# Mixture-of-experts layer of a fused decoder block: dense experts, or rows routed to slots by expert

## The reference

```
x = x + attn(layernorm(x))            # 16 heads of 64, 8 pooled "agent" queries a sequence
x = x + xattn(layernorm(x), ctx)      # 16 heads of 8, causal
x = x + ffn(layernorm(x))             # routed and shared experts
```

```
scores  = softmax(xf @ gate_w.T)                # 16 experts in 4 groups
idx     = the 2 best experts within the 2 best groups; weights = their scores
h       = silu(xf @ We1[e] + be1[e]) * (xf @ We3[e] + be3[e])       # 128 -> 64, an expert e
y       = sum over the 2 chosen e of weight * (h @ We2[e] + be2[e]) # 64 -> 128
z       = silu(xf @ ws1 + bs1) * (xf @ ws3 + bs3) @ ws2 + bs2       # shared, 128 -> 128 -> 128
return y + z
```

## Time and profile before

| what | value |
|---|---|
| median of 3 runs | 1166.43 us (1164.69 to 1166.88) |
| the profiled execution: its time, its span | 1165.22 us, 1163.5 us |
| busy in the span | PE 84%, PEld 66%, VectorE 68%, ScalarE 50%, GpSimd 20% |
| granted TensorE clock, mean | 0.921 |
| chain that ended last | PE 55%, VectorE 25%, ScalarE 12% |
| moved by DMA | 18.36 MB, 16 GB/s over the span |

### The profile page before, as it was taken

The page is one execution under the profiler, slowest core; times in us unless marked ns, Lnnn a source line. Parts: engine busy times, 40 slices in busy tenths (PEclk is TensorE's granted clock), DMA queues, the critical chain, the costliest instruction groups (busy, mean ns, idle before and its releaser), DMA issues.

```text
span 1163.5 us, 22091 instructions
## 1 busy us (share of the span) xinstructions
PE 975.4 (84%) x9023; PEld 768.2 (66%) x9069; DVE 791.6 (68%) x1841; ACT 576.3 (50%) x1148; POOL 227.7 (20%) x220
## 2 busy tenths in 40 slices
PE   6656889969897889978899698978899788996687
PEld 5543678737785577846787486855777477864566
DVE  3256866687766976678666877669766877568454
ACT  5335645357434664357453574346643574445322
POOL 6001410035000520024100340005200231004200
PEclk9896989979999999979899799989999899997789
DMA  5300010000100010000100000000100000000000
GB/s 145 78 1 1 2 37 1 10 10 6 33 10 10 2 37 1 10 10 2 37 10 1 10 26 13 10 10 2 37 1 10 11 2 1 10 2 10 1 1 19
DMA packets 28902, 18.36 MB, mean 16 GB/s; under 512 B 7649, under 2 KB 27394, under 8 KB 28802
## 3 DMA queue, kind: packets, MB, share of 16 engines
q1 hardware_dynamic: 26914, 12.48, 4.1%
q0 software_dynamic: 1280, 4.20, 1.2%
q10 hardware_dynamic: 608, 0.27, 0.1%
HBM read 12.62 MB, written 4.19 MB: 14 GB/s over the span
## 4 chain that ended last, share of the span: by engine, by line
PE 55%; DVE 25%; ACT 12%; POOL 3%; issue 3%; SPq 1%; DMA 0%; another core or an unknown queue 0%; DVEq 0%; POOLq 0%
PE banks L510 8%; PE banks L491 5%; PE banks L674 5%; PE banks L492 4%; PE banks L493 4%; DVE mx L1219 3%; PE banks L648 3%; PE banks L624 3%; DVE PXUT L1220 3%; ACT M L865 3%; PE banks L606 3%; PE banks L767 2%; DVE lx L1231 2%; PE banks L541 2%; DVE sil L1164 2%
## 5 line engine op out<-in xcount | busy, mean ns | idle before, releaser
L872 ACT ACTIVATE sil<-banks,b 128x512 f32<-128x512 f32 x144 | 99.6, 691 | 219.0 <-PE banks L493 216.8
L510 PE MATMUL banks<-w,hT 128*128 128x128 f32 x1152 | 156.8, 280 | 25.4 <-DVE hT L1171 22.8
L510 PEld LDWEIGHTS banks<-w,hT 128*128 128x128 f32 x1152 | 154.0, 196 | 22.2 <-DVE hT L1171 12.9
L1164 DVE SCALAR_TENSOR_TENSOR sil<-banks,b,sil 128x512 f32<-128x512 f32 x128 | 95.9, 749 | 103.1 <-ACT sil L872 94.2
L865 ACT COPY M<-banks 128x512 f32<-128x512 f32 x208 | 123.0, 609 | 81.0 <-PE banks L624 64.9
L389 POOL DMA_DIRECT2D out_x<-xn x16 | 12.9, 809 | 551.6 <-DVE xn L1177 551.6
L426 POOL TENSOR_TENSOR PXUT<-PXUT,rx 128x512 f32<-128x512 f32 x80 | 87.2, 1117 | 102.1 <-DVE rx L1233 102.1
L1171 DVE TENSOR_TENSOR hT<-sil,banks 128x512 f32<-128x512 f32 x128 | 87.9, 687 | 17.9 <-PE banks L500 11.4
L624 PE MATMUL banks<-ident,PXUT 128*128 128x128 f32 x384 | 64.4, 308 | 29.8 <-ACT M L865 24.0
L598 PE MATMUL banks<-maskb,pick 32*64 32x512 bf16 x512 | 45.0, 487 | 47.1 <-ACT PXUT L928 28.2
L624 PEld LDWEIGHTS banks<-ident,PXUT 128*128 128x128 f32 x384 | 45.4, 154 | 52.4 <-ACT M L865 34.2
(11 more groups left out here) (199 smaller groups left out, 2046.6 us busy)
## 6 DMA issues: line engine op xcount, KB each, us to landing
xin<-in_x SPq DMA_DIRECT2D x8, 512.0 KB, 4.2
cin<-in_ctx SPq DMA_DIRECT2D x8, 512.0 KB, 5.4
out_x<-xn POOLq DMA_DIRECT2D x16, 256.0 KB, 2.8
KQ<-in_L_attn_Wqkv SPq DMA_DIRECT2D x3, 512.0 KB, 5.3
KQ<-in_L_ffn_We SPq DMA_DIRECT2D x2, 512.0 KB, 4.5
KQ<-in_L_attn_Wo SPq DMA_DIRECT2D x1, 512.0 KB, 8.0
w<-in_L_ffn_We SPq DMA_DIRECT2D x1, 512.0 KB
woM<-xwT SPq DMA_DIRECT2D x16, 8.0 KB, 1.8
```

The costliest lines, as they stand in the source:

```text
L510: mm(ps(name)[:, P * t:P * t + P], hT[:, k % 2, P * t:P * t + P], w2[:, pair[k], :], start=(n == 0 and t == 0), stop=False, skip_group_che ...
L872: nc.scalar.activation(sil[:, k % 2, :], ps(f"H1_{k}")[:], ACT.Silu, bias=b1[:, pair[k]:pair[k] + 1]).then_inc(sil_ready, 1)
L1164: V.scalar_tensor_tensor(sil[:, k % 2, :], ps(f"H3_{k}")[:], b3[:, p:p + 1], sil[:, k % 2, :], ALU.add, ALU.mult).then_inc(hid_ready, 1)
```

## The change

The expert layer is computed for the chosen tokens only, and is spread over four rounds. The calls become `both(e, g, f, h)`, 11 of them: `g` is the attention's group, `e` one group behind (gate, shared experts, ranks), `f` two behind (experts), `h` three behind (sum).

For group `e`: the three-way split, `weight` and the dense units are removed. The shared experts are two fp32 chunks. `ranks` makes, by products with a triangle and with ones, each token's rank among its expert's tokens; `positions` on VectorE (16 linked instructions or so) turns these into a row number in a buffer of 32 slots of 128 rows, and into the expert of each slot (`ids`). GpSimd scatters `xn3` in 16 indirect DMAs of 128 rows to the buffer `xs_d` in HBM.

For group `f`: four units of 8 slots. SyncE reads each slot's expert from SBUF into a register and starts two DMAs by it (64 KB of `w13_d`, 33 KB of `w2b_d`), then loads the unit's rows (512 KB) and later stores the results (512 KB). TensorE turns the rows, multiplies (two slots share the array: 64 output rows each, then 64 input rows each), ScalarE and VectorE make silu and product on 128x128 pieces.

For group `h`: GpSimd gathers each token's two results in 16 indirect DMAs, VectorE adds them with their weights to `base`, which SyncE had stored and loads again.

```diff
-    UNITS = CHUNKS * (EP + 1)
+    SLOTS = TOPK * TOK // P + E
+    UNIT = 8
+    UNITS = SLOTS // UNIT
+    ROUNDS = GROUPS + 3
...
+            def weights(f, j):
+                n = UNITS * f + j
+                if n == 0:
+                    sp.wait_ge(packed, 16 * 5)
+                if n >= 2:
+                    sp.wait_ge(ys_ready, 2 * (n - 1))
+                for s in range(UNIT):
+                    row = UNIT * j + s
+                    e = sp.value_load(ids[row:row + 1, f % 2:f % 2 + 1], min_val=0, max_val=E - 1)
+                    sp.dma_start(w13[:, j % 2, s, :], w13_d[bass.ds(e, 1)].rearrange("a d i -> (a d) i")
+                                 ).then_inc(w_loaded[j % 2], 16)
+                    r = s % 2
+                    sp.dma_start(w2b[EI * r:EI * r + EI, j % 2, s // 2, :],
+                                 w2b_d[bass.ds(e, 1)].rearrange("a i d -> (a i) d")).then_inc(w_loaded[j % 2], 16)
+            def rows(f, j):
+                n = UNITS * f + j
+                if n >= 2:
+                    sp.wait_ge(ys_stored[j % 2], 16 * (n // 2))
+                sp.dma_start(xs[:, j % 2], xs_d[f % 2][P * UNIT * j:P * UNIT * (j + 1)].rearrange(
+                    "(s p) d -> p s d", p=P)).then_inc(xs_loaded[j % 2], 16)
+            def results(f, j):
+                sp.wait_ge(ys_ready, 2 * (UNITS * f + j) + 2)
+                sp.dma_start(ys_d[f % 2][P * UNIT * j:P * UNIT * (j + 1)].rearrange("(s p) d -> p s d", p=P),
+                             xs[:, j % 2]).then_inc(ys_stored[j % 2], 16)
+            def both(e, g, f, h):                        # SyncE
+                if h is not None:
+                    sp.wait_ge(base_stored, 16 * CHUNKS * (h + 1))
...
+                    sp.dma_start(base[:], o_v[h]).then_inc(base_loaded, 16)
+                if f is not None:
+                    sp.wait_ge(ids_ready, f + 1)
+                    weights(f, 0)
+                    sp.wait_ge(scattered, 16 * TOPK * T * (f + 1))
+                    rows(f, 0)
+                    weights(f, 1)
+                    rows(f, 1)
...
+                if f is not None:
+                    results(f, 0)
+                    weights(f, 2)
+                    rows(f, 2)
+                if h is not None:
+                    sp.wait_ge(summed, h + 1)
+                    sp.dma_start(o_v[h], base[:]).then_inc(stored, 16)
+                if f is not None:
+                    results(f, 1)
+                    weights(f, 3)
+                    rows(f, 3)
+                    results(f, 2)
+                    results(f, 3)
...
+            def both(e, g, f, h):                        # GpSimd, between xr and the second power
...
+                if h is not None:
+                    for k in range(2):
+                        pool.wait_ge(ys_stored[k], 8 * UNITS * (h + 1))
...
+                            pool.indirect_dma_start(          # 16 gathers
...
+                if e is not None:
+                    pool.wait_ge(pos_ready, e + 1)
...
+                            pool.indirect_dma_start(          # 16 scatters
...
+            def turn_rows(g, j):                         # TensorE
+                pe.wait_ge(xs_loaded[j % 2], 16 * ((UNITS * g + j) // 2 + 1))
+                for n in range(2):
+                    name = f"XS_{2 * j + n}"
+                    wait_free(pe, g, name)
+                    for s in range(4):
+                        last = turn_over(ps(g, name)[:, P * s:P * s + P], xs[:, j % 2, 4 * n + s, :], ident[:])
+                    last.then_inc(fulled(g, name), 1)
+            def expert_up(g, j):
+                pe.wait_ge(w_loaded[j % 2], 16 * 2 * UNIT * ((UNITS * g + j) // 2 + 1))
+                pe.wait_ge(xsT_ready, 2 * (UNITS * g + j) + 2)
...
```

More of the change, by code:

```diff
@@ L82, in decoder_block @@
+    place, before, fills = {}, {}, [0] * 8
+    for ring_banks, order in RINGS:
+        uses = []
+        for i in range(ROUNDS):
+            uses += [(name, i - lag) for lag, names in order for name in names if 0 <= i - lag < GROUPS]
+        for at, use in enumerate(uses):
+            k = ring_banks[at % len(ring_banks)]
+            fills[k] += 1
+            place[use] = (k, fills[k])
+            if at >= len(ring_banks):
+                before[use] = uses[at - len(ring_banks)]
     with ExitStack() as ctx:
@@ L752, in both @@
                     scores_2(g, 1)
-                    unit(e, 4)
-                    unit(e, 5)
+                if f is not None:
+                    expert_down(f, 0)
+                    expert_up(f, 1)
+                if g is not None:
                     turn_probs(g, 0)
-                    unit(e, 6)
+                if f is not None:
+                    turn_rows(f, 2)
+                if g is not None:
                     pool_tokens(g, 0)
                     turn_probs(g, 1)
-                    unit(e, 7)
+                if f is not None:
+                    expert_down(f, 1)
@@ L774, in both @@
                         for k in range(4):
[L775 to L777 removed]
+                            last = turn_over(ps(g, f"U_{n}")[:, P * k:P * k + P], UT[:, 4 * n + k, :], ident[:])
+                        last.then_inc(fulled(g, f"U_{n}"), 1)
+                if f is not None:
+                    expert_down(f, 2)
+                if g is not None:
@@ L795, in both @@
                     four(g, "xnT2_1", xn, 1)
-                unit(e, 16)
-                if g is not None:
                     for c in range(2):
@@ L811, in both @@
                     scores(g, 0)
-                if e is not None:
-                    down_to(e, 17)
-                if g is not None:
                     for u in range(UX):
@@ L989, in both @@
                         nc.scalar.activation(e2[:, q], e2[:, q], ACT.Exp, scale=AGENT_SCALE).then_inc(e2_ready, 1)
-                silu(e, 5)
+                if f is not None:
+                    results_moved(f, 0)
+                    expert_silu(f, 1)
                 if g is not None:
                     probs_moved(g, 0)
-                silu(e, 6)
+                if f is not None:
+                    rows_moved(f, 2)
                 if g is not None:
@@ L996, in both @@
                     probs_moved(g, 1)
-                silu(e, 7)
+                if f is not None:
+                    results_moved(f, 1)
                 if g is not None:
                     PX_moved(g, 1)
-                silu(e, 8)
+                if f is not None:
+                    expert_silu(f, 2)
                 if g is not None:
@@ L1004, in both @@
                         moved(g, f"UT_{n}", UT[:, :, h0:h0 + 4 * POOL].rearrange("p b (h i) -> p h b i", i=POOL),
-                              UT_ready, ps(f"UT_{n}")[:].rearrange("p (h b i) -> p h b i", b=GB, i=POOL))
-                silu(e, 9)
-                if e is not None:
-                    for n in range(2):
-                        moved(e, f"combT_{n}", combT[0:2 * E, 512 * n:512 * n + 512], combT_ready,
-                              ps(f"combT_{n}")[0:2 * E, :])
-                for k in range(10, 16):
-                    silu(e, k)
+                              UT_ready, ps(g, f"UT_{n}")[:].rearrange("p (h b i) -> p h b i", b=GB, i=POOL))
+                if f is not None:
+                    rows_moved(f, 3)
+                    results_moved(f, 2)
+                    expert_silu(f, 3)
+                    results_moved(f, 3)
                 if g is not None:
```

790 lines of the change are left out of this document (431 added, 359 removed).

## The result

| | before | after |
|---|---|---|
| median | 1165.56 us (1164.03 to 1166.88, 4 runs) | 1427.35 us (1426.79 to 1429.64, 4 runs) |
| span | 1163.5 us | 1426.0 us |
| granted TensorE clock, mean | 0.921 | 0.79 |

The ratio is 1.2251 [1.2234, 1.2268]: the changed kernel is 22.5% slower. The forecast was 1455 us, 2% above the result.

The account below looks back on a forecast made before the run. SyncE's in-order issue of each unit's weights (U, 14 us) was taken to decide: 1191 + 18U = 1443 us, plus 10 for TensorE's clock, and the median 3 above the span, forecast 1455 us, range 1290 to 1640.

Parts of the forecast that it names:

- stretches C and A: The rest of a round, from `QT` to the next `pooled`: 52 us, as before the change.
- U: SyncE's time to issue one unit's weights, 8 x (one register load + two DMAs): 14 us, ends 6.9 and 25.3.
- behind the last `QT`: After attention's last `QT`: 111 + 2U, then a round with experts alone 43 + 4U, then the last round 29 us.
- The mechanism: SyncE's queue: store, weights, then rows; TensorE stalls at units 2 and 3's rows, 19 and 15 to 20 us.
- the sum: Whole span, added over all rounds: 1191 + 18U = 1443 us.
- The arithmetic: TensorE, per round: 24 us of new work for 47 removed, alone saving up to 23 us.
- The first half of stretch B: From `pooled` to `turn_probs(0)`, in the stretch that `QT` ends: 41 us, against 39 before.
- the five rounds taken as full: Rounds with attention and slots, after the first two: 136 + 2U = 164 us each.
- The clock: TensorE's granted clock: longer idle stretches cost 1 to 2 us a round, 10 in all.
- TensorE's saving decides: Rival: unit 2's rows arrive in time, rounds take 127 us, sum 1124 us, faster than before; chance 0.07.
- SyncE or GpSimd much dearer: Rival: U above 20, or an indirect DMA above 3.2 us; 1560 us and up; chance 0.17.
- Packets: DMA engines: 23,500 packets of 512 to 520 bytes take 41 us a round; bandwidth isn't the bound.

Follow-up runs that it names:

- both edits: Against the changed kernel: rows of units 2 and 3 loaded ahead into `cin` and `xin`, and weights issued earlier in SyncE's queue; 1140.41 us, ratio 0.9792.
- no register loads: First experiment, against the changed kernel: slots take fixed experts, so DMAs have fixed addresses and SyncE reads no register; 1333.85 us, ratio 1.1454.
- two experiments: Fixed experts without register loads, against the changed kernel: 1333.85 us; expert read again for each 33 KB load, against the reordered kernel with rows ahead: 1228.36 us.
- the fastest kernel: Last experiment, against the reordered kernel with rows ahead: separate semaphore for 33 KB weights, first `w13` a round ahead, rows before weights; 1122.63 us, ratio 0.9627.

## Why the prediction was right

| step, us | predicted | measured |
|---|---|---|
| first `pooled`; first round; second round | 33; 98; 113 | 33.1; 97.4; 112.8 |
| stretches C and A | 52 | 52.5 |
| after `pooled`: ranks; unit 0's results moved | 27; 41 | 24.4; 36.5 |
| U, first and second trip of the round shown | 14 | 14.8; 16.2 |
| unit 2's rows; the stall before them | 60; 19 | 55.8; 18.3 |
| unit 3's rows; the stall before them | 93; 15 to 20 | 90.6; 21.5 |
| `QT`; the round | 112; 164 | 107.9; 160.4 |
| behind the last `QT`: 8th round, 9th, last | 139; 99; 29 | 145.6; 100.6; 33.6 |
| span | 1443 | 1426.0 |

**The mechanism** is shown. The same transfers in another order, with idle buffers for the rows, take 287 us less (both edits), and each microsecond of U costs some 17.5 us (no register loads), where the sum said 18. Both halves of the argument were needed, as put there: the weights behind the results, and the rows behind the weights.

**U.** The register load, for which no row stood, was taken at 0.65 us and is 0.52 to 0.68 by two experiments (0.60 and 0.59 in the single pairs shown); with the floor of the Trainium skill, "DMA: Bandwidth & Descriptors", Latency and other measured facts, some 600 ns, these roughly agree. The same page's fixed 2 us for each transfer, which its section Anatomy of one DMA gives for DMAs that GpSimd issues, would be an estimated 32 us for a unit if they came one after the other; here, on SyncE's queue, 16 went out in 14.8 us, so they overlap and the issue is what adds up. That part of a DMA's issue hides behind a load (0.37 against 0.58 us) is why U fell by some 5.3 us and not by 6.6 without loads, and why the first experiment was expected at 1307 us and took 1334. With the two DMAs at 1.12 us and the load, U lies 0.8 to 2 us above its 14.

**The arithmetic** saved 118.8 - 99.5 = 19 us of TensorE a round, and 21 where the clock is not lost to stalls (97.4); "up to 23" was right, and it was worth nothing here, being spent in stalls of 40 us.

**What was a little off.** The first half of stretch B was 4 us shorter than laid out, and with it rows, `QT` and the round. The first of the five rounds taken as full has no sum yet, and took 153.3 us and not 164: I had counted a wait for `summed` that isn't there. These and the four rounds give 30 us too much up to the last `QT`. The end was 13 us longer than its 267: a trip there takes 15 to 17 us, and 16 gathers at 1.25 us and their landing leave VectorE waiting for 28 us. So the total came within 2% in part by luck: 30 us too much up to the last `QT` stand against 13 too few behind it. The clock was put too low, at 1 to 2 us a round: after each stall the 8 transposes take 1.97 instead of 1.04 us, the 16 products of `pool_tokens` behind the first stall 2.08 us where the next 16 take 1.06, and `U` turned, behind the second, 3.27 instead of the 1.97 of the earlier trace rows. That is 4 us in the round shown, which the parts that were laid out too long covered.

**The rivals.** "TensorE's saving decides" was given 1124 us, if the chain of store, weights and rows were off the path. It was not, and the experiments that took it off came to 1140 and 1123, so the condition named there was the right one. That the number fits too is luck: the rival had rounds of 127 us and 170 us behind the last `QT`, and the fastest kernel has 118 and 218. "SyncE or GpSimd much dearer" fell: an indirect DMA is 0.95 to 1.0 us and 0.30 between two (I took 1.2), 53 us ahead of what waits for it. "Packets" fell: 512 KB still land in 4.2 us with 6.4 times the packets of before (185,403 against 28,902 in the run).

**Where my experiments' expectations failed.** For the kernel with both edits I expected 1186 us, with `QT` 80 us after `pooled`, and it was 70: with the rows there in time, the links of attention and the expert's units overlap more than my chain of handovers allowed; which of these links gave the 10 us was not traced. For the last I expected 1100 and got 1123, from counting on 20 us behind the last `QT` that SyncE's issue does not give.

**What stays open.** Behind the last `QT` even the fastest kernel needs 89 us more than before. What it would take with the weights issued by another engine's queue, with more buffers for them, or with fewer and larger loads, was not tried. That the 23 us between the fastest round, 118, and its 95 us of TensorE's work belong to attention's own handovers is argued and not shown.

## What to carry to other kernels

When data-dependent addresses come in, count what the issuing engine does in order, not the bytes: here a slot was one register load of some 0.6 us and two issues of 0.4 to 0.6 us, 1.8 us for 97 KB, and 8 of them stood between a store and a load that an idle TensorE waited for. Before giving up such a change, look for what can go ahead in that queue and for buffers that are idle just then: the same transfers took 1427 or 1140 us by their order and by which idle buffers they used. And price the rounds at the end, where a pipeline that is two stages deeper runs with nothing beside it: 152 of the 262 us were lost there, and 89 of them stayed in the best version.

## What the runs showed of the hardware that was not expected

- A register load on SyncE costs 0.52 to 0.68 us net, but the 64 KB DMA behind it issues in 0.37 us where it takes 0.58 without a load. It is as if the load hid some of the next issue; why was not tested.
- An issue costs about the same for 33 KB (0.45 to 0.49 us) as for 512 KB (0.37 to 0.59).
- An indirect DMA of 128 rows of 512 bytes keeps GpSimd for 0.96 us (gather) or 0.99 us (scatter) on average, and 0.30 more to the next.
- In the stalls of 18 and 20 us the granted clock was 0.58 and 0.52 on average, and the first 8 transposes behind each took 1.97 us, twice those before them. Over these transposes the granted clock was 0.50: TensorE came back at the lower of its two levels, 1.2 GHz.
